# Six inverse roots of norms as one power on GpSimd

## What is computed

```python
def _layernorm(x, axis=-1, eps=1e-05):
    m = jnp.mean(x, axis=axis, keepdims=True)
    v = jnp.var(x, axis=axis, keepdims=True)
    return (x - m) / jnp.sqrt(v + eps)
def _rmsnorm(v, w):
    return v * jax.lax.rsqrt(jnp.mean(v * v, axis=-1, keepdims=True) + EPS_RMS) * w
def _srms(x, d):
    rms = jnp.linalg.norm(x, axis=-1, keepdims=True) * d ** (-0.5)
    return x / (rms + EPS)
h = _L0_tok_ref(x, L0_tok_W)                                   # embedding and positions
h = h + _L0_attn_ref(_layernorm(h), ...)                       # linear attention
h = h + _L0_ffn_ref(_layernorm(h), ...)                        # causal attention, then 8 experts, each behind an _rmsnorm
h = h + _L1_attn_ref(_layernorm(h), ...)                       # mixing by Fourier transforms, with an _srms at its end
h = h + _L1_ffn_ref(_layernorm(h), ...)                        # one projection
```

## Time and profile before

| | us |
|---|---|
| median of 3 runs | 383.98 |
| the three runs | 380.18, 384.93, 383.98 |
| the profiled execution | 387.35 |
| its span, first to last instruction | 385.6 |
| TensorE busy in the span | 333.8 (87%) |
| VectorE | 237.0 (61%) |
| ScalarE | 144.2 (37%) |
| GpSimd | 105.1 (27%) |

### The profile page before, as it was taken

One profiled execution on the slowest core, in us unless ns is written; L12 is line 12 of the kernel. 1 busy time (PEld: TensorE's weight loads), 2 busy tenths in 40 slices (PEclk: granted clock), 3 DMA queues, 4 the chain that ended last, 5 costly groups with the idle time before them and its releaser, 6 DMA issues.

```text
span 385.6 us, 4537 instructions
## 1 busy us (share of the span) xinstructions
PE 333.8 (87%) x1675; PEld 184.8 (48%) x1675; DVE 237.0 (61%) x394; ACT 144.2 (37%) x238; POOL 105.1 (27%) x137
## 2 busy tenths in 40 slices
PE   1357877959899989778999999999989999899995
PEld 0124655522334442444775455554645555467744
DVE  1498775879887750115578455565467667764385
ACT  2123437330575658332156345554352112012260
POOL 5795000235421222200000142121001788900000
PEclk9998998975899999856979999999999999999998
DMA  7949200076000000000000000000000000000001
GB/s 273 300 147 417 116 0 0 2 121 126 1 3 0 2 4 0 2 0 0 2 0 1 0 2 0 3 0 0 3 0 2 0 0 2 0 0 0 2 1 54
DMA packets 6167, 15.27 MB, mean 40 GB/s; under 512 B 1282, under 2 KB 3714, under 8 KB 5506
## 3 DMA queue, kind: packets, MB, share of 16 engines
q1 hardware_dynamic: 5410, 14.27, 11.8%
q0 software_dynamic: 512, 0.53, 0.6%
q10 hardware_dynamic: 224, 0.20, 0.4%
HBM read 12.05 MB, written 0.52 MB: 33 GB/s over the span
## 4 chain that ended last, share of the span: by engine, by line
PE 64%; DVE 19%; ACT 7%; POOL 5%; issue 3%; DMA 1%; ACTq 0%; SPq 0%; DVEq 0%
PE ps L301 62%; DVE share L1268 2%; POOL e_lo L418 1%; DVE st L1224 1%; DVE arena L1467 1%; DVE rw L1400 1%; DMA idt<-ident 1%; PE ps L498 1%; DVE st L1231 1%; DVE xc L1232 1%; DVE sq L1240 1%; ACT arena L1045 1%; ACT sq L973 1%; POOL arena L484 1%; ACT L979 1%
## 5 line engine op out<-in xcount | busy, mean ns | idle before, releaser
L301 PE MATMUL ps<-arena 96*128 96x512 bf16 (+6 forms) x192 | 48.6, 362 | 5.2 <-DMA arena<-arena 3.6
L1092 ACT ACTIVATE arena<-ps 128x1024 f32<-128x1024 f32 (+3 forms) x48 | 37.9, 812 | 36.9 <-PE ps L301 36.2
L1400 DVE TENSOR_REDUCE rw<-ps 128x1 f32<-128x512 f32 (+3 forms) x78 | 45.7, 643 | 7.8 <-PE ps L301 7.8
L301 PE MATMUL ps<-bfc_s 128*128 128x512 bf16 (+2 forms) x173 | 44.3, 371 | 1.1 <-DVE tmp L1365 1.1
L301 PE MATMUL ps<-xs,e_hi 128*128 128x512 f32 x96 | 41.0, 427 | 0.2 <-ACT arena L1118 0.2
L1467 DVE TENSOR_TENSOR arena<-ps,arena 128x512 f32<-128x512 f32 x48 | 33.0, 691 | 11.2 <-ACT arena L1118 10.8
L301 PE MATMUL ps<-xs,e_lo 128*128 128x512 f32 x96 | 38.9, 406 | 0.0
L1118 ACT ACTIVATE arena<-ps 128x512 f32<-128x512 f32 x48 | 28.7, 598 | 26.1 <-PE ps L301 22.4
L301 PEld LDWEIGHTS ps<-arena 96*128 96x128 bf16 (+1 forms) x192 | 16.5, 103 | 37.0 <-DVE rw L1400 18.6
L301 PE MATMUL ps<-share,tu_s 128*128 128x384 f32 x96 | 32.5, 488 | 0.0
L301 PE MATMUL ps<-w,xT 128*128 128x128 f32 (+3 forms) x160 | 27.1, 357 | 3.0 <-DVE xT L1430 1.6
(11 more groups left out here) (236 smaller groups left out, 501.1 us busy)
## 6 DMA issues: line engine op xcount, KB each, us to landing
w<-wpack SPq DMA_DIRECT2D x1, 2152.5 KB, 10.5
arena<-arena SPq DMA_DIRECT2D x22, 96.0 KB, 2.8
arena<-tm SPq DMA_DIRECT2D x2, 1024.0 KB, 5.9
arena<-epack SPq DMA_DIRECT2D x1, 1540.0 KB, 11.1
arena<-rope SPq DMA_DIRECT2D x1, 1024.0 KB, 13.3
tu_s<-tu SPq DMA_DIRECT2D x2, 512.0 KB, 12.1
tk_s<-tk SPq DMA_DIRECT2D x2, 512.0 KB, 13.6
rp<-rpack SPq DMA_DIRECT2D x1, 678.5 KB, 4.1
```

The costliest lines, as they stand in the source:

```text
L301: return nc.tensor.matmul(o, l, r, start=start, stop=stop, **kw)
L1092: nc.scalar.activation(pt[:, n % PT_SLOTS, :, lo:512], ps[:, bank:bank + 2, lo:512], ACT.Exp, scale=HD ** -0.5).then_inc(S("exp_done"), 1)
L1400: V.tensor_reduce(top_view(m, part)[:, at:at + len(heads), i], src, AXX, ALU.max, negate=True).then_inc(S("ring_read"), 1)
```

## The change

The root and the reciprocal of six norms (all but var1) become one instruction on GpSimd: `tensor_tensor` with the operation pow, 128 x 16, of the mean squares and of a constant tile that holds -0.5. For var3b the exponent is 0.5, and VectorE's addition of 1e-8 and its reciprocal remain. Six activations on ScalarE, five reciprocals on VectorE and nine of the twelve `next_function` calls go. Two memsets of 128 x 16 on GpSimd are added. The division by D1 in var3b moves from the activation's scale into VectorE's copy.

```diff
+        powers = sb("powers", [P, 2, NT * B])
@@ GpSimd
+            def root(norm, dst, src, power=0):
+
+                pool.wait_ge(S("mean_squares"), NORMS[norm])
+                nc.gpsimd.tensor_tensor(dst, src, powers[:, power], ALU.pow).then_inc(S("roots"), 1)
+
...
+            for k, power in enumerate((-0.5, 0.5)):
+                nc.gpsimd.memset(powers[:, k], power).then_inc(S("powers"), 1)
             nc.gpsimd.memset(geo[:], 0.0).then_inc(S("constants"), 1)
...
             nc.gpsimd.tensor_copy(uvb[64:96], left[64:96]).then_inc(S("bias_pieces"), 1)
+            pool.wait_ge(S("powers"), 2)
+            pool.wait_ge(S("bias_pieces"), 1)
+            root("var2", st[:, 4], st[:, 2])
+            root("msq2", st[:, 7], st[:, 5])
...
+            root("var2b", st[:, 4], st[:, 2])
...
+            root("var3", st[:, 4], st[:, 2])
...
+            root("var3b", st[:, 3], st[:, 2], 1)
+            root("var4", st[:, 4], st[:, 2])
@@ ScalarE, in the six norms (here var3)
-            next_function(ACT.Sqrt)
-
             squares(3, xc)
-            act.wait_ge(S("mean_squares"), NORMS["var3"])
-            nc.scalar.activation(st[:, 3], st[:, 2], ACT.Sqrt).then_inc(S("roots"), 1)
-            next_function(ACT.Silu)
@@ VectorE, in five norms (here var3)
             centre(3, S("mean_squares"), add_bank(h, 0, S("moe")))
             dve.wait_ge(S("roots"), NORMS["std3"])
-            step(V.reciprocal(st[:, 4], st[:, 3]))
             scale_rows(x1, xc, 4, S("n3"))
@@ VectorE, var3b
-            V.tensor_copy(st[:, 2], st[:, 1]).then_inc(S("mean_squares"), 1)
+            V.tensor_scalar(st[:, 2], st[:, 1], 1.0 / D1, None, ALU.mult).then_inc(S("mean_squares"), 1)
```

More of the change, by code:

```diff
@@ L1031, in _ @@
                     squares(1, xc)
-                    act.wait_ge(S("mean_squares"), NORMS["var2"])
-                    nc.scalar.activation(st[:, 3], st[:, 2], ACT.Sqrt).then_inc(S("roots"), 1)
[L1034 to L1037, removed]
             evac(2, S("T2"), 1, S("xT2_lo"), scale=W("ln1"))
@@ L1102, in _ @@
                 nc.scalar.activation(sq[:, 4 * a:4 * a + 4], x1[:, 4 * a:4 * a + 4], ACT.Square).then_inc(S("squared"), 1)
-            act.wait_ge(S("mean_squares"), NORMS["var2b"])
-            nc.scalar.activation(st[:, 3], st[:, 2], ACT.Sqrt).then_inc(S("roots"), 1)
-            next_function(ACT.Exp)
             for b in range(B):
@@ L1164, in _ @@
             squares(4, xc)
-            act.wait_ge(S("mean_squares"), NORMS["var3b"])
-            nc.scalar.activation(st[:, 3], st[:, 2], ACT.Sqrt, scale=1.0 / D1).then_inc(S("roots"), 1)
-            next_function(ACT.Silu)
             for a in range(2):
@@ L1171, in _ @@
                 nc.scalar.activation(v, v, ACT.Silu).then_inc(S("xr"), 1)
-            next_function(ACT.Sqrt)
             squares(5, xc)
-            act.wait_ge(S("mean_squares"), NORMS["var4"])
-            nc.scalar.activation(st[:, 3], st[:, 2], ACT.Sqrt).then_inc(S("roots"), 1)
             evac(2, S("T4"), 1, S("xT4_lo"))
@@ L1353, in _ @@
             dve.wait_ge(S("roots"), NORMS["rms2"])
-            step(V.reciprocal(st[:, 7], st[:, 6]))
             scale_rows(sq, x1, 7, S("n2"))
```

## The result

The changed kernel takes 404.3 us (median of 4 runs, 400.95 to 410.3) against 384.46 for the kernel before (median of 4, 380.18 to 385.28). The ratio is 1.050, with a 95% interval of 1.040 to 1.060: slower, and outside the range on record. The profiled execution took 404.6 us with a span of 402.9, 17.3 us more than the span before.

A forecast was written before the change was run, and what follows sets the result against it. The chain that ended last was 64% TensorE, 19% VectorE, 7% ScalarE. The norms' terms summed to 5p - 1.90, +2.6 us at p = 0.9, giving 386.6 us from the median 383.98; range for 8 in 10: 381.5 to 394.

The forecast's parts named there:

- The size of p: Duration of one GpSimd power on 16 numbers per partition: taken as 0.9 us, with ends 0.216 and 2.3.
- 6p - 3.04: Predicted added us over the six norms for p above 1.14; below that the sum is 5p - 1.90.
- rival 1: The power on GpSimd is slow: decides from p = 1.8, 7.7 us; with p = 3, +15, 399 us. Chance 20%.
- The table loads: Of the loads taken out, only the one in var3b is on the chain, worth some 0.2 us; the others nothing.
- The rule of the drain: A table switch on ScalarE costs some 2.66 us including a drain; by that the change brings about 5 us more.
- The norm terms: Added us per norm: var2 and var3 p - 0.44, msq2 p - 0.28, var4 p - 0.43, var3b p - 0.31, var2b nothing.
- the cover: At var2b, TensorE's fixed row of matmuls hides 0.7 us of added time, used up at p = 1.14.
- msq2 held up by VectorE: Second root of the var2 norm: its power waits for VectorE's multiplication, so p - 0.28; side by side, -0.28.
- GpSimd's queue: Roots and other work in GpSimd's queue don't delay each other; the rival that a root waits: below 1 us, 2%.
- rival 3: TensorE's clock falls earlier, between 283 and 290, behind var3: 3 us more, 389.6. Chance 12%.

## Why the prediction was wrong

- *The size of p* is the step that failed. I took 0.9 us from a guess of 20 passes at 35 ns; the power takes 2.90 to 2.96 us, 70 additions per element and not 20. The sum nearly held: 6p - 3.04 at p = 2.93 is 14.5 us, and the norms' stretches grew by 13.6. The span grew by 17.3, and most of the other 3.7 goes with the clock; the medians are 19.8 apart, and what of the last 2.5 is more than scatter isn't known. It was rival 1, which decides from p = 1.8. I gave it 20% and cut the range at p = 2.2, although my own words were that nothing in the trace bounds p from above. With such a term the range has to reach further, or the forecast has to rest on something other than short rows of another operation.
- *The table loads*: right. Nine went, one was on the chain, worth 0.12 us (I had said 0.2), and of the others nothing can be seen. ScalarE's busy time fell by 14.2 us for nothing, 14.7 forecast. The rule of the drain, from the Trainium skill's "ScalarE: Activation LUTs", section "What ACT_TABLE_LOAD costs", would have made them worth some 5 us; taking the loads out showed no such gain.
- *The norm terms*: right to 0.1 us each, but for var2b. There the formula gives +1.8 at the measured p, and the norm cost 1.0. I had counted the cover from the last split to the end of the keep_warm row, 0.85 us, as if all sixteen transposes waited for that split. Eight of the sixteen wait only for the first one and stand between the row and those that need the last: the cover is 1.5 us and not 0.7, and it is used up at about p = 1.9 and not 1.14.
- *msq2 held up by VectorE*: right for the order that the kernel has, 3.81 us recorded for a power of 2.9. The rule that I set beside it, the Trainium skill's "SBUF — State Buffer", section "SBUF: two separate sides", of an exclusive lock held for a whole instruction, agrees with this order; it does not fit the other one, where both ran together (1.23 us for the multiplication inside a power of 2.90).
- *GpSimd's queue*: right, no other work was late; with a cheap operation in the same places the loss was gone.
- *The clock* (rival 3, 12%): it came, at the very place named, on top of rival 1 and not in place of it. I priced it at 3 us; behind var3 it cost 7.0, because the half-speed stretch lasted 17 us and not only the 5.9 us of work in the window that I had looked at. It was also more likely than I had said, since TensorE's idle time grew to over 3 us with the longer power.
- *Against it* the profiled execution won back 4.6 us before var2b. Whether the change did that is open. With no power in var2 and msq2 seven of nine traces have the 20.5 us at half speed around 160 to 183, the two others 6.8 and 13.7 us of it; with the power there none of four has it whole (3.4 to 13.7), and the stretch up to var2b takes 111.9 to 115.0 us in them for 116.4 to 116.8 in the seven. I had no term for a clock that recovers elsewhere, and no run was made to test it.

## What to carry to other kernels

An operation that no row of the trace shows has no upper bound from rows of other operations; before it goes on a chain of short dependent steps, measure it alone, in idle time, at two sizes. Table loads are worth what waits behind them, which here was 0.12 us of the 13.4 that nine loads with their dummies take. A longer wait on another engine can also cost TensorE's clock in the work behind it: lengthen the keep_warm row with the wait, and read the granted clock of the whole next stage, not of its first microseconds. Work that is made in halves is covered half by half: look for the instruction that waits for the last half before you count a cover.

## What the runs showed of the hardware

- A power on GpSimd costs about 0.35 to 0.4 us and 0.16 us for each element per partition (2.9 us for 128x16, 10.5 for 128x64); an addition or product of 128x16 costs 0.22.
- GpSimd's power was held up by a VectorE multiplication with two operands in SBUF that was under way (3.81 us recorded for 2.9, and 1.13 for 0.22 with a product in its place), but such a multiplication that came 0.1 us after a power's start ran in its usual 1.23 us.
- Half-speed stretches of TensorE lasted from 3.4 to 20.5 us, some through stretches in which TensorE was busy all the time: 7.00 of 7.00 us between 289 and 296, at a granted clock of 0.56. Behind 3.3 to 3.4 us of idle time ahead of var3 the clock was at half for 17.1 to 20.5 us in three of three traces, behind 0.9 us or less in none of ten.
- The kernel before ranges over 2.5% in unchanged form (380.0 to 389.5 us), the long times with the low mean granted clocks (0.959 to 0.925).
